# A top-k search on VectorE: two pairs of a head kept aside, and one of its two lists searched past the eighth entry

## Chip, core and metric

The kernel runs on one core of one Trainium2 chip. The metric is device time in microseconds (us) of one execution. The core's engines are TensorE (PE in the profile, with PEld for its weight loads), VectorE (DVE), ScalarE (ACT), GpSimd (POOL) and the DMA queue that SyncE (SP) issues. Each engine works through its own list of instructions in order and waits on semaphores for the others.

## What is computed

The input is 8192 tokens of width 256 (2 sequences of 4096). A first phase is an attention-like layer with layer norms, which the change doesn't touch. The second phase is a layer of product-key experts, and the change lies in its selection of experts. Cut to what matters:

```python
q = (x @ Wq + bq).reshape(B, S, N_HEADS, D_QUERY)            # 8 heads, 64 wide
q1, q2 = q[..., :DQ_HALF], q[..., DQ_HALF:]
s1 = jnp.einsum('bshd,nd->bshn', q1, K1)                     # 64 scores
s2 = jnp.einsum('bshd,nd->bshn', q2, K2)                     # 64 scores
v1, i1 = jax.lax.top_k(s1, TOPK)                             # TOPK = 10
v2, i2 = jax.lax.top_k(s2, TOPK)
all_scores = v1[..., :, None] + v2[..., None, :]             # 10 x 10 sums
all_indices = i1[..., :, None] * N_SQRT + i2[..., None, :]
vals, best = jax.lax.top_k(all_scores, TOPK)
expert_idx = jnp.take_along_axis(all_indices, best, axis=-1)
scores = jax.nn.softmax(vals, axis=-1)
h = jax.nn.gelu(jnp.einsum('bsd,bshkd->bshk', x, W_down[expert_idx]), approximate=False) * scores
out = jnp.einsum('bshk,bshkd->bsd', h, W_up[expert_idx])
```

The experts in use number 4096. The kernel doesn't gather their rows: it multiplies every token with all of them, and with a matrix of gates that is zero where an expert wasn't chosen.

## The kernel before

**Phases.** `attention_phase` runs until about 800 us of the span. `experts_phase` follows and works in 32 chunks of 256 tokens (`C`; two tiles `t` of 128 tokens, `NT` = 2). It is a pipeline over the chunks, written out by hand: in round m (the loops `for m in range(-3, chunks + 1)` of every engine) the engines work on chunk m for the experts' matmuls, on chunk m+1 for the gate matrix, on chunk m+2 for the top-k search, and on chunk m+3 for the queries and scores.

**PE in a round** (lines 1217 to 1237). Sixteen times a `down` (L1201: 12 matmuls, hidden values of 256 experts into PSUM banks `b_ps_h`), and three steps behind it an `up` (L1212: 8 matmuls into `b_ps_a`). Then `turn_x`, `queries` (L1176), `sum_picks` (L1149, needs VectorE's `product`), `scores` (L1186), `turn_picks` (L1157) and four blocks of `gate_matrix` (L1126), each of 128 matmuls with one-hot factors `ohq` and `ohr`. Block b needs `ohr` of that block from VectorE; `ohr` has two buffers, so VectorE may write that of block 2 only once PE is through block 0.

**ACT in a round.** A `gelu` (L1360) for each `down`, one-hots of block 1 (L1339, L1347), then `turn_x`, `keep_gate_parts` (L1316: two copies into a PSUM bank `b_ps_h`, which the factors `ohr` are made from; it has to wait for the last `gelu`), queries, scores (L1298) into `b_score`, the exponential of the softmax (L1304), and the copies of the gate matrix (L1247).

**POOL in a round.** `norm_in` of chunk m+3, then sixteen times a `mix` (L1028: gelu times gates, which `up` of that step waits for) and thirteen times a part of the one-hots of block 0 (L1043). At step 10 come `numbers` (L1059, L1060, the indices of the lists as numbers; it waits for the lists of both tiles) and `pair_numbers` (L1069, L1072, the expert number `cid` of each candidate).

**VectorE in a round** (lines 1612 to 1646). `moments_in`, `decode`; then, for chunk m+2, `lists_first` and `lists_rest` of tile 0 and of tile 1. There are 16 lists of 64 scores (8 heads, two lists each) in a tile. `lists_first` takes the eight largest of each list (L1502) and their indices (L1506). `lists_rest` overwrites these eight (L1513), takes the next eight (L1517) and their indices (L1521), so that ten are known. `pair_sums` (L1540, five instructions) adds the 27 pairs of entries that can be among the ten best into `b_cand`. `pairs_top` does with these 27 what was done with the lists, in five steps of 8 instructions for each tile (L1551, L1555, L1559, L1563, L1567). Then `shift` (L1597), `mask` (L1573, L1581: a comparison over 4320 fp16 elements) and `product` (L1590, the same size, needs `cid`). After that comes chunk m+1: `keep_q_numbers` (L1422), `ohr` of blocks 0 and 1 (L1433, L1438, L1440 each; L1438 waits for `keep_gate_parts`), `ohq` of block 2 (L1412), `finish` (L1480), `ohq` of block 3, `ohr` of block 2 (waits for PE's block 0), `norm_out` (L1489), `ohr` of block 3, `soften` (L1603 to L1607).

The maximum, find-index and match-replace instructions of VectorE work on one list of one head each; find-index and match-replace load the eight values first (MATCH_VALUE_LOAD).

## Time and profile before

| | |
|---|---|
| median of 3 runs | 3499.29 us (3498.52 to 3501.48) |
| the profiled execution | 3501.89 us, its span 3500.1 us |
| mean granted TensorE clock | 0.897 of full speed |
| PE busy | 3179.7 us, 91% of the span |
| DVE busy | 2952.2 us, 84% |
| ACT busy | 2138.9 us, 61% |
| POOL busy | 1916.9 us, 55% |

These shares are means over the attention phase, the two rounds in which the expert pipeline fills, 30 rounds in which all chunks are in work, and the end. Each of these has to be read by itself: which engine's waits end last there. A duration in the trace is that of one instruction from its start to its end; instructions that follow each other on an engine overlap by some 0.1 us, so that a chain of short ones is shorter than the sum of its durations. "issue" as the releaser of a wait means that the profile shows none.

### The profile page before, as it was taken

To read this page: it belongs to the slowest core of one execution; us is meant where nothing else is said; L and a number is where in the kernel's file an instruction comes from. 1 tells how busy PE (TensorE), PEld (TensorE's weight loads), DVE (VectorE), ACT (ScalarE), POOL (GpSimd) and SP (SyncE) were. 2 spreads that over 40 slices of the span, in tenths; PEclk is the share of its full clock that TensorE was granted. 3 is DMA by queue.
4 is the path that set the end of the run, shared out by engine and by line. 5 is a ranking of instruction groups with operands and counts; after the bars stand their busy time and mean duration, and the time that the engine had idled before them with its cause. 6 is when DMAs were issued, how large, how long until landed. Compare 5 with 4: busy or idle time off the path is not lost. (4 is left out here: it accounts for less than half of the span.)

```text
span 3500.1 us, 91378 instructions
## 1 busy us (share of the span) xinstructions
PE 3179.7 (91%) x31284; PEld 2737.6 (78%) x31284; DVE 2952.2 (84%) x15052; ACT 2138.9 (61%) x4475; POOL 1916.9 (55%) x1758
## 2 busy tenths in 40 slices
PE   5999999982499999999999999999999999999998
PEld 3666666641388888888888888888888888888887
DVE  4566666655999999999999999999999999999942
ACT  3444444421677777766766776677667767776762
POOL 1333333332466666665556666666655566666652
PEclk9999999985699999999988899999999889999988
DMA  2111111103333333333333333333333333433332
GB/s 65 49 55 55 55 55 48 45 29 121 125 122 130 119 122 116 107 123 118 107 107 107 124 126 123 121 119 107 116 125 107 107 107 123 127 123 121 116 122 88
DMA packets 132329, 356.86 MB, mean 102 GB/s; under 512 B 13865, under 2 KB 61609, under 8 KB 129452
## 3 DMA queue, kind: packets, MB, share of 16 engines
q1 hardware_dynamic: 131868, 351.03, 31.0%
q8 instruction: 251, 4.11, 0.5%
q14 instruction: 210, 1.72, 0.2%
...
## 5 line engine op out<-in xcount | busy, mean ns | idle before, releaser
L1212 PE MATMUL b_ps_a<-b_wup,b_hid 128*128 128x256 f32 x4096 | 955.7, 379 | 0.0
L1201 PE MATMUL b_ps_h<-b_xT_hi,b_wd_split 128*128 128x256 f32 x4096 | 936.6, 313 | 19.6 <-ACT b_hid L1360 19.5
L1028 POOL TENSOR_TENSOR b_hid<-b_hid,b_gates 128x512 f32<-128x512 f32 x512 | 768.3, 1501 | 182.9 <-ACT b_hid L1360 182.5
L1212 PEld LDWEIGHTS b_ps_a<-b_wup,b_hid 128*128 128x128 f32 x4096 | 744.3, 190 | 84.0
L1201 PEld LDWEIGHTS b_ps_h<-b_xT_hi,b_wd_split 128*128 128x128 f32 x4096 | 707.2, 201 | 35.4 <-issue 24.9
L1339 ACT ACTIVATE b_ohq<-b_q_no,b_minus_qid 80x128 f16<-80x128 f16 x2048 | 648.4, 390 | 1.0
L1201 PE MATMUL b_ps_h<-b_xT_lo,b_wd_split 128*128 128x256 f32 x2048 | 598.9, 292 | 0.0
L1126 PE MATMUL b_ps_s<-b_ohr,b_ohq 80*128 80x32 f16 x16384 | 452.4, 185 | 106.9 <-issue 66.1
L1126 PEld LDWEIGHTS b_ps_s<-b_ohr,b_ohq 80*128 80x128 f16 x16384 | 443.6, 102 | 115.9 <-issue 72.3
L1360 ACT ACTIVATE b_hid<-b_ps_h 128x512 f32<-128x512 f32 x512 | 304.0, 594 | 372.2 <-PE b_ps_h L1201 372.2
L1043 POOL TENSOR_TENSOR b_ohq<-b_qT 80x640 f16<-80x640 f16 (+1 forms) x416 | 520.4, 1252 | 0.0
L1201 PEld LDWEIGHTS b_ps_h<-b_xT_lo,b_wd_split 128*128 128x128 f32 x2048 | 413.9, 202 | 9.9
L1247 ACT ACTIVATE b_gates<-b_ps_s 128x512 f32<-128x512 f32 x512 | 298.4, 596 | 184.7 <-PE b_ps_s L1126 182.0
L1009 POOL TENSOR_SCALAR b_rstd<-b_mv 128x2 f32<-128x2 f32 x64 | 14.1, 221 | 518.1 <-DVE b_mv L1402 518.1
L1347 ACT ACTIVATE b_ohq<-b_ohq,b_one 80x1024 f16<-80x1024 f16 x256 | 291.6, 1139 | 0.0
L1412 DVE TENSOR_TENSOR b_ohq<-b_qid,b_ps_h 80x8192 f16<-80x8192 f16 x64 | 281.4, 4397 | 0.0
L240 POOL TENSOR_TENSOR a_ret<-a_prod 128x512 f32<-128x512 f32 x64 | 84.9, 1327 | 329.6 <-DVE a_prod L618 329.6
L1017 POOL TENSOR_TENSOR b_y<-b_y,b_x1t 128x512 f32<-128x512 f32 x32 | 40.7, 1273 | 303.6 <-DVE b_y L1489 303.6
L1433 DVE TENSOR_TENSOR b_ohr<-b_rid,b_ps_h 80x2048 f16<-80x2048 f16 x128 | 155.2, 1213 | 57.1 <-PE b_ps_s L1126 56.0
L1506 DVE FIND_INDEX8 b_idx<-b_val,b_score 128x8 uint16<-128x64 f32 x1024 | 200.4, 218 | 0.0
L1521 DVE FIND_INDEX8 b_idx<-b_val,b_score 128x8 uint16<-128x64 f32 x1024 | 200.4, 219 | 0.0
L1513 DVE MATCH_REPLACE8 b_score<-b_val,b_score 128x64 f32<-128x64 f32 x1024 | 199.7, 209 | 0.0
...
## 6 DMA issues: line engine op xcount, KB each, us to landing
b_wd_split<-wd_parts SPq DMA_DIRECT2D x512, 512.0 KB, 4.0
...
```

The lines of the kernel that those rows point to most:

```text
L1028: G.tensor_tensor(hid[:, p % 4, :, :], hid[:, p % 4, :, :], gates[:, 2 * p:2 * p + 2, :], ALU.mult).then_inc(mix_done, 1)
L1043: G.tensor_tensor(ohq[:, tok, :].rearrange("p n (a b) -> p n a b", a=16), oh16[:, tok, :].unsqueeze(3).to_broadcast(shape), oh8[:, tok, :] ...
L1126: mm = T.matmul(bank[:, n * NR:(n + 1) * NR], ohq[:, tok, :], ohr[:, b % 2, tok - b * BLK, part, :], start=part == 0, stop=part == 1)
L1201: mm = T.matmul(hbank[p % 2][:, j * C:(j + 1) * C], a, c, start=i == 0, stop=i == len(parts) - 1)
L1212: mm = T.matmul(abank[:, t * D:(t + 1) * D], hid[:, p % 4, j, t * P:(t + 1) * P], wup[:, 2 * p + j, :], start=p == 0 and j == 0 and t == 0 ...
L1247: S.mul(gates[:, :, g * GROUP:(g + 1) * GROUP], sbank[fills["gates", m, g] % 3][:, :].rearrange("p (n r) -> p r n", r=NR), 1.0 / GATE_SCAL ...
L1339: op = S.activation(ohq[:, BLK + i, :], q_no[0:SLOTS, :], ACT.Abs, bias=minus_qid[:, i:i + 1])
L1347: S.activation(rows, rows, ACT.Relu, bias=one[:, :], scale=-1.0).then_inc(ohq_act_done, 1)
L1360: S.activation(hid[:, p % 4, :, :], hbank[p % 2][:, :].rearrange("p (j c) -> p j c", j=2), ACT.Gelu).then_inc(gelu_done, 1)
L1412: V.tensor_tensor(ohq[:, tok, :].rearrange("p n (q s) -> p n q s", s=2), qid[:, tok, :].unsqueeze(2).to_broadcast(shape), q_no_ps.rearrang ...
L1506: op = V.max_index(idx[:, t, l, 0:8], val[:, t, l, 0:8], src(l))
L1521: op = V.max_index(idx[:, t, l, 8:16], val[:, t, l, 8:16], src(l))
```

## The change

On the 16 lists of a tile `lists_first` is unchanged, but both tiles are now done first. A new step `choose` then adds, for each head, the first entry of list 1 and the third of list 2, and the eighth entry of list 1 and the first of list 2, and compares the two sums. By the comparison either list 1 or list 2 of a head is searched further: where it is the second, its scores are copied over those of the first with a predicated copy (64 elements for each of 16 heads and tiles), and its eight values likewise. `lists_rest` then works on 8 lists instead of 16 in a tile. A new step `place_rest` puts the two further entries in the place of both lists and sets them to -3e38 in the one that wasn't searched. POOL's `numbers` waits for it.

`pairs_top` now searches for eight of the 27 pairs only, in two steps instead of five. A new step `sure_pairs` before it takes out two pairs that are certain: the sum of the two first entries, and the larger of the sums (first, second) and (second, first). It writes them into places 8 and 9 of the result and overwrites them in `b_cand`. The order of the ten chosen experts changes by this, which their sum doesn't depend on; `shift` subtracts the value in place 8 instead of that in place 0.

The diff, without empty lines:

```diff
--- before.py
+++ after.py
@@ -37,6 +37,7 @@
 AT_GLO, AT_CID = 5, 10
 ACT_PARTS = 8
 NQ_ACT = NQ
+SURE = 8
 CA = 512
 TA = CA // P
@@ -829,6 +830,8 @@
     id1 = sb("b_id1", [P, HEADS, TOPK, NT], F16)
     id2 = sb("b_id2", [P, HEADS, TOPK, NT], F16)
     cand = sb("b_cand", [P, NT * HEADS, NPAIR], F32)
+    ends, absent, second = cand[:, :, 0:2], cand[:, :, 2:4], cand[:, :, 4].bitcast(mybir.dt.uint32)
     cid = sb("b_cid", [P, HEADS, NPAIR, NT], F16)
     posf = sb("b_posf", [P, SLOTS, NT], F16)
     picked = sb("b_picked", [P, SLOTS, WIDE, NT], F16)
@@ -836,6 +839,7 @@
     pos = picked[:, :, :, :].rearrange("p s c t -> p (s c t)")[:, 0:NT * HEADS * 16].bitcast(U16).rearrange(
         "p (l k) -> p l k", k=16)
     gate = sb("b_gate", [P, NT, SLOTS], F32)
+    won = sb("b_won", [P, NT * HEADS, 2], F32)
     gsum = sb("b_gsum", [P, NT * HEADS], F32)
     ghi = sb("b_ghi", [SLOTS, C, 2], F16)
@@ -894,6 +898,8 @@
     pairs_done = [sem(f"b_pairs{i}") for i in range(NT)]
     ids_done, cand_done, posf_done, mask_done, picks_done = (sem(f"b_{n}") for n in ("ids", "cand", "posf", "mask", "picks"))
     shift_done, gsum_done, grecip_done, gate_done = (sem(f"b_{n}") for n in ("shift", "gsum", "grecip", "gate"))
+    choice_done = sem("b_choice")
+    sure_done = sem("b_sure")
     q_no_done, eid_done, fields_done, qid_done, id16_done, oh16_done = (
         sem(f"b_{n}") for n in ("q_no", "eid", "fields", "qid", "id16", "oh16"))
     ohr_eq_done, ohr_hi_done, ohr_lo_done, ohq_done, q_no_ps_done = (
@@ -1052,8 +1058,7 @@
         def numbers(m):
             i = idx[:, :, :, 0:TOPK].rearrange("p t (h s) k -> p h s k t", s=2)
-            pool.wait_ge(lists_done[0], 5 * (m + 1))
-            pool.wait_ge(lists_done[1], 5 * (m + 1))
+            pool.wait_ge(choice_done, 4 * (m + 1))
             if m:
                 pool.wait_ge(cid_done, m)
             G.tensor_scalar(id1[:, :, :, :], i[:, :, 0, :, :], float(NSQ), -2048.0, ALU.mult, ALU.add)
@@ -1506,20 +1511,53 @@
                 op = V.max_index(idx[:, t, l, 0:8], val[:, t, l, 0:8], src(l))
             op.then_inc(lists_done[t], 1)
+        def choose(m):
+            v = val.rearrange("p t (h s) k -> p (t h) s k", s=2)
+            s = score.rearrange("p t (h s) n -> p (t h) s n", s=2)
+            for t in range(NT):
+                dve.wait_ge(lists_done[t], 5 * m + 2)
+            V.tensor_copy(v[:, :, 0, 8:16], v[:, :, 0, 0:8])
+            V.tensor_tensor(ends[:, :, 0], v[:, :, 0, 0], v[:, :, 1, 2], ALU.add)
+            V.tensor_tensor(ends[:, :, 1], v[:, :, 0, 7], v[:, :, 1, 0], ALU.add).then_inc(choice_done, 1)
+            dve.wait_ge(choice_done, 4 * m + 1)
+            V.tensor_tensor(second, ends[:, :, 0], ends[:, :, 1], ALU.is_ge)
+            V.tensor_tensor(absent[:, :, 0], ends[:, :, 0], ends[:, :, 1], ALU.is_ge)
+            V.tensor_tensor(absent[:, :, 1], ends[:, :, 0], ends[:, :, 1], ALU.is_lt).then_inc(choice_done, 1)
+            dve.wait_ge(choice_done, 4 * m + 2)
+            V.copy_predicated(v[:, :, 0, 8:16], second.unsqueeze(2).to_broadcast([P, NT * HEADS, 8]), v[:, :, 1, 0:8])
+            V.copy_predicated(s[:, :, 0, :], second.unsqueeze(2).to_broadcast([P, NT * HEADS, NSQ]),
+                              s[:, :, 1, :]).then_inc(choice_done, 1)
         def lists_rest(m, t):
-            src = lambda l: score[:, t, l, :]
-            dve.wait_ge(lists_done[t], 5 * m + 2)
-            for l in range(LISTS):
-                op = V.match_replace(src(l), val[:, t, l, 0:8], src(l), GONE)
+            src = lambda h: score[:, t, 2 * h, :]
+            dve.wait_ge(choice_done, 4 * m + 3)
+            for h in range(HEADS):
+                op = V.match_replace(src(h), val[:, t, 2 * h, 8:16], src(h), GONE)
             op.then_inc(lists_done[t], 1)
             dve.wait_ge(lists_done[t], 5 * m + 3)
-            for l in range(LISTS):
-                op = V.max(val[:, t, l, 8:16], src(l))
+            for h in range(HEADS):
+                op = V.max(val[:, t, 2 * h + 1, 8:16], src(h))
             op.then_inc(lists_done[t], 1)
             dve.wait_ge(lists_done[t], 5 * m + 4)
-            for l in range(LISTS):
-                op = V.max_index(idx[:, t, l, 8:16], val[:, t, l, 8:16], src(l))
+            for h in range(HEADS):
+                op = V.max_index(idx[:, t, 2 * h + 1, 8:16], val[:, t, 2 * h + 1, 8:16], src(h))
             op.then_inc(lists_done[t], 1)
+        def place_rest(m):
+            v = val.rearrange("p t (h s) k -> p (t h) s k", s=2)
+            i = idx.rearrange("p t (h s) k -> p (t h) s k", s=2)
+            for t in range(NT):
+                dve.wait_ge(lists_done[t], 5 * m + 5)
+            V.tensor_copy(i[:, :, 0, 8:TOPK], i[:, :, 1, 8:TOPK])
+            for s in range(2):
+                op = V.scalar_tensor_tensor(v[:, :, s, 8:TOPK], absent[:, :, s:s + 1].to_broadcast([P, NT * HEADS, TOPK - 8]), GONE,
+                                            v[:, :, 1, 8:TOPK], ALU.mult, ALU.add)
+            op.then_inc(choice_done, 1)
         def moments_in(m):
             dve.wait_ge(x1_in, 16 * (m + 1))
@@ -1532,48 +1570,53 @@
         def pair_sums(m):
             v = val[:, :, :, :].rearrange("p t (h s) k -> p (t h) s k", s=2)
-            dve.wait_ge(lists_done[0], 5 * (m + 1))
-            dve.wait_ge(lists_done[1], 5 * (m + 1))
-            if m:
-                dve.wait_ge(pairs_done[1], 5 * m)
+            dve.wait_ge(choice_done, 4 * (m + 1))
+            if m:
+                dve.wait_ge(pairs_done[1], 2 * m)
             for a0, na, nb, off in PAIRS:
                 op = V.tensor_tensor(cand[:, :, off:off + na * nb].rearrange("p h (a b) -> p h a b", a=na),
                                      v[:, :, 0, a0:a0 + na].unsqueeze(3).to_broadcast([P, NT * HEADS, na, nb]),
                                      v[:, :, 1, 0:nb].unsqueeze(2).to_broadcast([P, NT * HEADS, na, nb]), ALU.add)
             op.then_inc(cand_done, 1)
+        def sure_pairs(m):
+            first, either = cand[:, :, 0:1], cand[:, :, 1:11:9]
+            s01, s10 = cand[:, :, 1:2], cand[:, :, 10:11]
+            dve.wait_ge(cand_done, m + 1)
+            V.tensor_tensor(won[:, :, 0:1], s01, s10, ALU.is_ge)
+            V.tensor_tensor(won[:, :, 1:2], s01, s10, ALU.is_lt)
+            V.tensor_copy(top[:, :, SURE:SURE + 1], first)
+            V.tensor_tensor(top[:, :, SURE + 1:TOPK], s01, s10, ALU.max).then_inc(sure_done, 1)
+            dve.wait_ge(sure_done, 2 * m + 1)
+            V.memset(first, GONE)
+            V.tensor_scalar(posf[:, :, :].rearrange("p (h k) t -> p t h k", k=TOPK)[:, :, :, SURE + 1],
+                            won[:, :, 0].rearrange("p (t h) -> p t h", t=NT), -9.0, 10.0, ALU.mult, ALU.add)
+            V.scalar_tensor_tensor(either, won[:, :, :], GONE, either, ALU.mult, ALU.add).then_inc(sure_done, 1)
         def pairs_top(m, t):
             src = lambda h: cand[:, t * HEADS + h, :]
             vals = lambda h: top[:, t * HEADS + h, :]
             ids = lambda h: pos[:, t * HEADS + h, :]
-            dve.wait_ge(cand_done, m + 1)
+            dve.wait_ge(sure_done, 2 * m + 2)
             for h in range(HEADS):
                 op = V.max(vals(h)[:, 0:8], src(h))
             op.then_inc(pairs_done[t], 1)
-            dve.wait_ge(pairs_done[t], 5 * m + 1)
+            dve.wait_ge(pairs_done[t], 2 * m + 1)
             for h in range(HEADS):
                 op = V.max_index(ids(h)[:, 0:8], vals(h)[:, 0:8], src(h))
             op.then_inc(pairs_done[t], 1)
-            dve.wait_ge(pairs_done[t], 5 * m + 2)
-            for h in range(HEADS):
-                op = V.match_replace(src(h), vals(h)[:, 0:8], src(h), GONE)
-            op.then_inc(pairs_done[t], 1)
-            dve.wait_ge(pairs_done[t], 5 * m + 3)
-            for h in range(HEADS):
-                op = V.max(vals(h)[:, 8:16], src(h))
-            op.then_inc(pairs_done[t], 1)
-            dve.wait_ge(pairs_done[t], 5 * m + 4)
-            for h in range(HEADS):
-                op = V.max_index(ids(h)[:, 8:16], vals(h)[:, 8:16], src(h))
-            op.then_inc(pairs_done[t], 1)
         def mask(m):
-            dve.wait_ge(pairs_done[NT - 1], 5 * (m + 1))
+            dve.wait_ge(pairs_done[NT - 1], 2 * (m + 1))
             for t in range(NT):
-                op = V.tensor_copy(posf[:, :, t].rearrange("p (h k) -> p h k", h=HEADS),
-                                   pos[:, t * HEADS:(t + 1) * HEADS, 0:TOPK])
+                op = V.tensor_copy(posf[:, :, t].rearrange("p (h k) -> p h k", h=HEADS)[:, :, 0:SURE],
+                                   pos[:, t * HEADS:(t + 1) * HEADS, 0:SURE])
             op.then_inc(posf_done, 1)
             dve.wait_ge(posf_done, m + 1)
+            dve.wait_ge(q_no_done, 1)
             if m:
                 dve.wait_ge(picks_pe, m)
             dve.wait_ge(lists_done[0], 5 * (m + 1))
@@ -1591,11 +1634,11 @@
                 [P, HEADS, TOPK, NPAIR * NT]), ALU.mult).then_inc(picks_done, 1)
         def shift(m):
-            dve.wait_ge(pairs_done[NT - 1], 5 * (m + 1))
+            dve.wait_ge(pairs_done[NT - 1], 2 * (m + 1))
             if m:
                 dve.wait_ge(gate_pe, m)
             V.tensor_tensor(gate[:, :, :].rearrange("p t (h k) -> p (t h) k", k=TOPK), top[:, :, 0:TOPK],
-                            top[:, :, 0:1].to_broadcast([P, NT * HEADS, TOPK]), ALU.subtract).then_inc(shift_done, 1)
+                            top[:, :, SURE:SURE + 1].to_broadcast([P, NT * HEADS, TOPK]), ALU.subtract).then_inc(shift_done, 1)
         def soften(m):
             g4 = gate[:, :, :].rearrange("p t (h k) -> p (t h) k", k=TOPK)
@@ -1607,6 +1650,8 @@
             V.tensor_tensor(g4, g4, gsum[:, :].unsqueeze(2).to_broadcast([P, NT * HEADS, TOPK]), ALU.mult).then_inc(gate_done, 1)
         dve.wait_ge(consts_in, 16 * N_CONSTS)
+        V.memset(posf[:, :, :].rearrange("p (h k) t -> p h k t", k=TOPK)[:, :, SURE, :], 0.0)
         V.tensor_scalar(q_no[:, :], minus_q, -1.0, None, ALU.mult).then_inc(q_no_done, 1)
         for m in range(-3, chunks + 1):
@@ -1616,11 +1661,13 @@
                 decode(m + 1)
             if has(m + 2):
                 lists_first(m + 2, 0)
-            if has(m + 2):
+                lists_first(m + 2, 1)
+                choose(m + 2)
                 lists_rest(m + 2, 0)
-                lists_first(m + 2, 1)
                 lists_rest(m + 2, 1)
+                place_rest(m + 2)
                 pair_sums(m + 2)
+                sure_pairs(m + 2)
                 pairs_top(m + 2, 0)
                 pairs_top(m + 2, 1)
                 shift(m + 2)
```

## Rows read from the trace of the kernel before

**Rows 1.** The page's table of engines: busy us, share of span, instructions.

```profile
PE 3179.7 (91%) x31284; PEld 2737.6 (78%) x31284; DVE 2952.2 (84%) x15052; ACT 2138.9 (61%) x4475; POOL 1916.9 (55%) x1758
```

**Rows 2.** Waits: who waited for whom, us in total, times, longest.

```profile
DVE b_ohr L1433 <- PE b_ps_s L1126: 56.0, 29, 2.0
PE b_ps_s L1126 <- issue: 66.1, 67, 8.4
```

**Rows 3.** Timeline of VectorE, one round: start us, duration us, line, operation.

```profile
2004.70 2.11 DVE L1502 MAX8 b_val<-b_score 128x8 f32<-128x64 f32 x16
...
2010.10 0.09 DVE L1513 MATCH_VALUE_LOAD b_score<-b_val,b_score 128x8 f32 x1
...
2018.62 2.10 DVE L1502 MAX8 b_val<-b_score 128x8 f32<-128x64 f32 x16
...
2032.69 2.00 DVE L1540 TENSOR_TENSOR b_cand<-b_val 128x160 f32<-128x160 f32 x5
2034.73 0.81 DVE L1551 MAX8 b_val<-b_cand 128x8 f32<-128x27 f32 x8
...
2038.33 0.81 DVE L1563 MAX8 b_val<-b_cand 128x8 f32<-128x27 f32 x8
...
2040.43 0.78 DVE L1551 MAX8 b_val<-b_cand 128x8 f32<-128x27 f32 x8
...
2049.27 3.37 DVE L1590 TENSOR_TENSOR b_score<-b_score,b_cid 128x4320 f16<-128x4320 f16 x1
...
2054.06 1.22 DVE L1438 TENSOR_TENSOR b_ohr<-b_ohr,b_ps_h 80x2048 f16<-80x2048 f16 x1
...
2071.68 1.22 DVE L1433 TENSOR_TENSOR b_ohr<-b_rid,b_ps_h 80x2048 f16<-80x2048 f16 x1 [1.93 <-PE b_ps_s L1126]
...
2084.90 2.11 DVE L1502 MAX8 b_val<-b_score 128x8 f32<-128x64 f32 x16
```

**Rows 4.** Timeline of ACT, the second copy of `keep_gate_parts` in that round.

```profile
2053.47 0.36 ACT L1316 COPY b_ps_h<-b_glo 80x256 f32<-80x256 f32 x1
```

**Rows 5.** Timeline of PE in that round, after the last `down`.

```profile
2051.82 5.35 PE L1212 MATMUL b_ps_a<-b_wup,b_hid 128*128 128x256 f32 x24
...
2060.46 2.31 PE L1149 MATMUL b_ps_m<-b_score,b_ident 128*128 128x480 f16 x9
```

**Rows 6.** Timeline of POOL in that round.

```profile
2012.73 1.28 POOL L1028 TENSOR_TENSOR b_hid<-b_hid,b_gates 128x512 f32<-128x512 f32 x1
...
2032.86 1.33 POOL L1043 TENSOR_TENSOR b_ohq<-b_qT 80x640 f16<-80x640 f16 x1
...
2050.54 3.24 POOL L1028 TENSOR_TENSOR b_hid<-b_hid,b_gates 128x512 f32<-128x512 f32 x1 [0.17 <-ACT b_hid L1360]
```

**Rows 7.** One instruction of `pair_sums`, 2033.3 to 2034.0: min/median/max ns.

```profile
L1540 DVE TENSOR_TENSOR b_cand<-b_val x1: 1294/1294/1294, 2033.0 to 2033.0; 128x80 f32<-128x80 f32 x1
```

**Rows 8.** Groups by line of VectorE: xcount, busy us, mean ns, idle before.

```profile
L677 DVE SCALAR_TENSOR_TENSOR a_ph<-a_turns,a_ph 128x1024 f32<-128x1024 f32 x24 | 29.4, 1225 | 0.8
...
L1448 DVE TENSOR_SCALAR b_field<-b_eid 80x64 uint16<-80x64 uint16 x32 | 5.7, 177 | 1.1
```

**Rows 9.** Timeline of VectorE while the pipeline fills.

```profile
853.59 1.18 DVE L1540 TENSOR_TENSOR b_cand<-b_val 128x160 f32<-128x160 f32 x5
...
929.15 2.41 DVE L1590 TENSOR_TENSOR b_score<-b_score,b_cid 128x4320 f16<-128x4320 f16 x1
```

**Rows 10.** Timeline of PE while the pipeline fills.

```profile
871.79 3.78 PE L1149 MATMUL b_ps_m<-b_score,b_ident 128*128 128x480 f16 x9 [28.56 <-DVE b_score L1590]
...
951.48 4.70 PE L1126 MATMUL b_ps_s<-b_ohr,b_ohq 80*128 80x32 f16 x162 [5.31 <-issue]
```

**Rows 11.** Timeline of ACT while the pipeline fills.

```profile
924.38 0.36 ACT L1316 COPY b_ps_h<-b_glo 80x256 f32<-80x256 f32 x1
```

**Rows 12.** Timeline of ACT in the last round with a top-k search.

```profile
3335.40 0.36 ACT L1316 COPY b_ps_h<-b_glo 80x256 f32<-80x256 f32 x1
```

**Rows 13.** Timeline of VectorE in that round.

```profile
3337.52 1.22 DVE L1438 TENSOR_TENSOR b_ohr<-b_ohr,b_ps_h 80x2048 f16<-80x2048 f16 x1
```

## Prediction

> **What bounds the kernel now.** I began with the table of engines [rows 1]: PE is busy for 91% of the span, VectorE for 84%. These are means over stages, and in the expert phase both are near full, so the table decides nothing. The waits do [rows 2]. VectorE waits for PE 29 times, 56.0 us in all: in 29 of the rounds it stands still 1.9 us before `ohr` of block 2, until PE is through block 0 of the gate matrix. PE's own waits in that stage come to 66.1 us "issue" over 67 times, the longest 8.4 us. Then I read one round in VectorE's timeline [rows 3]. It begins its lists at 2004.70 and again at 2084.90, so a round takes 80.20 us. Everything between follows without a gap, except 1.93 us before 2071.68.
>
> That gap is the point to see. VectorE arrives at it early, and leaves it when PE allows. What lies behind it (`ohr` 2, `norm_out`, `ohr` 3) starts from PE's block 0 and not from VectorE's own past. In front of it there is a second tie: the multiplication at 2054.06 needs the copies of ACT, the second of which starts at 2053.47 and takes 0.36, so ends at 2053.83 [rows 3, 4]. VectorE begins 0.23 us after that. However early `product` ends, `ohr` can't be ahead of now by more than 0.23 us, and even this is only added to a wait that exists. `product` itself ends at 2052.64 (2049.27 + 3.37), and PE takes it up at 2060.46, after its queries [rows 3, 5]: 7.8 us of slack. So the filled pipeline runs at PE's pace, with VectorE 1.93 us from being the bound. The search can become some 12 us shorter without a gain there, and may become at most 1.93 us longer.
>
> It is otherwise in three places. While the pipeline fills, PE waits 28.56 us for the first `product` [rows 10]: the whole search of chunk 0 is exposed. In the next round PE waits 5.31 us at block 2, at 951.48, for VectorE, which has worked without a pause since its second search; `product` ended there at 931.56, and ACT's copies at 924.74 [rows 9 to 11], so that tie is far off. In the last round with a search ACT's copies end at 3335.76 and VectorE multiplies at 3337.52 [rows 12, 13]: it is 1.76 us behind, and here nothing waits for PE, since no queries and scores delay PE's block 0.
>
> **The change part by part, without contention.**
> - Removed from the lists: `lists_rest` of a tile takes 8.52 us (2010.10 to 2018.62 [rows 3]), and half of its instructions go. Two tiles: 8.5 us.
> - Removed from the pairs: five steps take 5.70 us a tile (2034.73 to 2040.43), the last two of them 2.10 (2038.33 to 2040.43) [rows 3]. Two steps stay, so 2 x 3.60 = 7.2 us go. Together 15.7.
> - Added: 17 short instructions (7 in `choose`, 3 in `place_rest`, 7 in `sure_pairs`, of 16 to 128 elements) and one predicated copy of 1024 elements. A short one lasts 0.18 us alone, but starts 0.1 us after its forerunner; the nearest row is L1448 with 177 ns [rows 8]. I take 0.12 each, 2.0 us; the ends are 1.3 and 3.0. The wait for its own results that VectorE makes six times costs about 0.12 each, 0.7 us. The trace of before has no predicated copy. L677, with two inputs and 1024 elements, takes 1225 ns [rows 8], and that I take; at two elements a step it would be 0.7, at two passes 2.4. Sum 3.9 us, between 2.7 and 6.1.
> - Net: 15.7 - 3.9 = 11.8 us less in a search, if nothing stands in the way.
> - `lists_first` of tile 1 comes some 8.5 us earlier; its scores were copied in the round before. POOL's `numbers` now waits for `place_rest`, which ends before POOL gets there at its step 10. Behind it stand the `mix` instructions of steps 11 to 15; with contention, below, the two meet within about 1 us, and the `mix` has 3 us or more of slack. The memset ahead of the loop costs nothing that can be read.
>
> **The contention.** One instruction of `pair_sums`, 80 elements, took 1294 ns in the filled pipeline [rows 7], while POOL's one-hots ran from 2032.86 to 2034.19 [rows 6]. All five together took 1.18 us at 853.59, where POOL had little to do, and 2.00 in the round shown [rows 3, 9]. So an instruction with two inputs in SBUF lets the running one of POOL end first, up to 1.2 us, and POOL in turn takes 3.24 us instead of 1.3 for a `mix` that meets `product` [rows 6]. In the part where `choose` falls, from about 2015.4, POOL runs such instructions back to back [rows 6].
>
> The Trainium skill says the same in "SBUF — State Buffer", section "Who interferes with whom": VectorE and GpSimd share a port pair, and "Whoever issues first gets the shared pair for the whole instruction; the other fully blocks". It counts an instruction with two SBUF inputs among those that meet it and a plain copy in a two-port mode too. That speaks against this change, which puts many small ones of this kind where there were few big ones without; taken to its end it gives the first rival below.
>
> About 20 of the instructions in `choose`, `place_rest`, `pair_sums` and `sure_pairs` have two inputs or copy. Between two of POOL's there is a gap of 0.1 us, into which one or two short ones fit. Stepping both queues through with the durations above, I find six waits in `choose`: its copy (0.8), the first sum (1.1), the second with the first comparison (1.0), the other two (1.1), and each predicated copy (1.0), together 6.1. Behind it there are 1.9 in `place_rest`, 1.9 in `pair_sums`, and 1.7 in `mask` and `product`: 11.6 us in all, where before it was 0.8 in `pair_sums` and 1.0 in `product` (3.37 against 2.41 [rows 3, 9]). That eats about 10 of the 11.8 us. `product` then ends 1 to 2 us earlier than now, VectorE waits for ACT's copies or for PE as before, and the round stays at 80.2 us: 30 rounds x 0. POOL's last `mix` ended at 2053.78, while the last 8 of PE's 24 matmuls, which need it, start at about 2055.4 (2051.82 + 5.35 x 16/24) [rows 5, 6]. The two big comparisons now fall before steps 13 and 14 and cost POOL two waits of 2.4; I find 1 us of slack left at step 14.
>
> **The sum.** Chunk 0: POOL is nearly idle after 838, so of 11.8 us one or two waits go (1.3): 10.5 us gained, all of it on the path, since everything up to ACT's second half of preparing weights starts from there. Chunk 1: POOL prepares weights and one-hots back to back, `choose` costs 6.1 more and the rest 1.5: 4.2 us gained (0 to 8.2, the latter up to the tie with ACT's copies). Last search: 1.2 us of the possible 1.76. Together 15.9 us. From the profiled execution's 3501.9 that gives 3486.0; it was 2.6 us above the median of 3499.3, so the forecast for the median is 3484 us with rounding.
>
> **The rivals.**
> - *The port makes VectorE the bound.* If each instruction that meets POOL waits for a whole one, and no two fit in a gap, my steps put the end of `product` 1.1 to 3.7 us later than now. It decides from 1.93 us on, the gap of rows 3, that is from 13.7 us more waiting than now. At 3.2 us late a round costs 1.2 us more, 30 x 1.2 = 36, and the gains left are 10.5 + 0.5: 3499 + 25 = 3524. At the far end (3.7) it is 30 x 1.8 - 10 = 44, 3543. For it: rows 7, a full wait of an instruction that followed another directly. Against it: only one of five waited in that round.
> - *POOL gets late.* With `mask` and `product` ahead of `mix` 13 and 14, `up` waits on PE. If the `mix` is 1 us beyond its slack, 30 x 1 - 15.9 = +14: 3513. It decides from 1 us on.
> - *Nothing at the start either.* If the search of chunk 0 hides another bound (the weights' preparation and its DMAs), 10.5 becomes about 3 and the total is 4 to 6: 3494. The 28.56 us of PE's wait speak against it.
> - *VectorE was the bound.* If the rounds follow VectorE, 1 to 2 us less in 30 rounds give 45 more: 3440. The 29 waits of VectorE for PE speak against it.
>
> **How the numbers follow.** Forecast (fill and end only): 0.68. Port: 0.12. POOL late: 0.07. Nothing at the start: 0.10. VectorE the bound: 0.03. The forecast's own bounds are 3476 (11.8 + 8.2 + 1.8 = 21.8, with 1 us for shorter instructions) and 3492. The range takes in the third rival and small losses in the rounds, up to 0.5 us each: 3476 to 3500. What a measurement can tell from no change is about 0.2%, 7 us. Below 3492.3 lie the forecast and the last rival: 0.70. The third rival and a forecast whose gain is eaten by small losses: 0.14. Slower: 0.16.
>
> **What the profile after would show.** The wait of PE for the first `product` falls from 28.56 to about 18 us; the one at block 2 in the next round from 5.31 to about 2 or 3; rounds still of 80.2 us; VectorE waiting for ACT's copies or PE in each round; three or more of the short instructions of `choose` at over 1 us; the group of `lists_rest` halved. Wrong would be: rounds longer than 80.5, no wait of VectorE before `ohr` 2 (first rival), or PE waiting at L1212 for POOL (second).

## The result, and the profile after

The changed kernel takes 3635.34 us (median of 4 runs, 3634.3 to 3638.24), the kernel before 3499.44 (4 runs, 3498.52 to 3501.48). The ratio is 1.0387, with a 95% interval of 1.0373 to 1.0401: 136 us slower, where 15 us faster was forecast. The first rival happened (the port makes VectorE the bound), at five times its price (136 us against 25): it gave 3524, at its far end 3543.

The page of the changed kernel, its table of engines:

```profile
PE 3180.8 (88%) x31284; PEld 2734.2 (75%) x31284; DVE 3140.7 (86%) x10509; ACT 2138.5 (59%) x4475; POOL 1859.0 (51%) x1758
```

Against [rows 1] PE does the same work in the same time (3180.8 and 3179.7 us). VectorE has 30% fewer instructions (10509 against 15052) and is busy for 189 us more. POOL is busy for less. So short instructions have become long ones on VectorE: one that waits for POOL shows no idle time before it, but a long duration, and counts as busy.

The waits of the changed kernel: who waited for whom, us in total, times, longest.

```profile
PE b_ps_s L1131 <- issue: 182.5, 67, 9.6
DVE b_ohr L1438 <- PE b_ps_s L1131: 2.9, 5, 0.6
PE b_ps_a L1217 <- POOL b_hid L1034: 17.3, 23, 0.8
POOL b_id L1064 <- DVE b_val L1558: 166.8, 32, 11.6
```

These are the mirror image of [rows 2]. VectorE's 29 waits for PE (56.0 us) are down to 5 (2.9 us), and PE's own in the gate stage went from 66.1 to 182.5 us. VectorE had 1.93 us to spare in a round; now PE waits for it. POOL stands before its `numbers` instruction 32 times, 166.8 us in all.

One round in VectorE's timeline (start, duration in us, line, operation), from the first list search to the next, without its own long searches:

```profile
2047.91 2.11 DVE L1507 MAX8 b_val<-b_score 128x8 f32<-128x64 f32 x16
...
2058.64 2.32 DVE L1523 COPY b_val<-b_val 128x128 f32<-128x128 f32 x1
2060.87 1.28 DVE L1524 TENSOR_TENSOR b_cand<-b_val 128x16 f32<-128x16 f32 x1
2062.07 2.55 DVE L1525 TENSOR_TENSOR b_cand<-b_val 128x16 f32<-128x16 f32 x1
2064.66 2.31 DVE L1527 TENSOR_TENSOR b_cand<-b_cand 128x16 uint32<-128x16 f32 x1
2066.88 1.32 DVE L1528 TENSOR_TENSOR b_cand<-b_cand 128x16 f32<-128x16 f32 x1
2068.12 2.56 DVE L1529 TENSOR_TENSOR b_cand<-b_cand 128x16 f32<-128x16 f32 x1
2070.71 2.54 DVE L1531 COPY_PREDICATED b_val<-b_cand,b_val 128x128 f32<-128x128 uint32 x1
2073.15 2.37 DVE L1532 COPY_PREDICATED b_score<-b_cand,b_score 128x1024 f32<-128x1024 uint32 x1
...
2084.53 0.18 DVE L1556 COPY b_idx<-b_idx 128x32 uint16<-128x32 uint16 x1
2084.62 0.29 DVE L1558 SCALAR_TENSOR_TENSOR b_val<-b_cand,b_val 128x32 f32<-128x32 f32 x2
2084.94 1.19 DVE L1577 TENSOR_TENSOR b_cand<-b_val 128x160 f32<-128x160 f32 x5
...
2091.61 2.62 DVE L1640 TENSOR_TENSOR b_gate<-b_val 128x160 f32<-128x160 f32 x1
2094.15 4.97 DVE L1615 CAST b_posf<-b_picked 128x64 f16<-128x64 uint16 x2
2099.16 2.41 DVE L1624 TENSOR_TENSOR b_score<-b_posf,b_pair_no 128x4320 f16<-128x4320 f16 x1
2101.60 2.41 DVE L1633 TENSOR_TENSOR b_score<-b_score,b_cid 128x4320 f16<-128x4320 f16 x1
...
2134.25 2.11 DVE L1507 MAX8 b_val<-b_score 128x8 f32<-128x64 f32 x16
```

The round takes 86.34 us (2134.25 - 2047.91), against 80.20 [rows 3]. The eight instructions of `choose` take 16.9 us (2058.64 to 2075.52); five of them touch 16 elements a partition and last 1.3 or 2.3 to 2.6 us each. Behind `pairs_top`, `shift` (L1640) takes 2.62 us and the two casts of `mask` (L1615) 4.97 us, both unchanged operations, where they take 0.32 and 0.31 while the pipeline fills (at 906.63). `place_rest` and `pair_sums` (2084.53 to 2086.13) wait for nothing. `product` ends at 2104.01, which is 56.1 us after the round's start; before, it was 47.94 (2052.64 - 2004.70, [rows 3]).

POOL's timeline in the same stretch:

```profile
2062.06 1.27 POOL L1049 TENSOR_TENSOR b_ohq<-b_qT 80x640 f16<-80x640 f16 x1
2063.27 1.30 POOL L1034 TENSOR_TENSOR b_hid<-b_hid,b_gates 128x512 f32<-128x512 f32 x1
...
2085.00 0.48 POOL L1064 TENSOR_SCALAR b_id<-b_idx 128x160 f16<-128x160 uint16 x1 [5.74 <-DVE b_val L1558]
...
2094.01 3.81 POOL L1034 TENSOR_TENSOR b_hid<-b_hid,b_gates 128x512 f32<-128x512 f32 x3
```

The second sum (L1525, 2062.07 to 2064.62) starts 0.01 us after a one-hot of POOL, which ends at 2063.33. It doesn't get in there: it lasts until POOL's next instruction, a `mix`, ends at 2064.57. The `numbers` instruction (L1064) has waited 5.74 us for `place_rest`; meanwhile three `mix` instructions have become due, which run back to back from 2094.01 to 2097.82, and POOL's next instruction follows them until 2099.05. The two casts (2094.15 to 2099.12) end with that one.

PE's timeline at the end of the round, block 2 of the gate matrix:

```profile
2124.85 3.58 PE L1131 MATMUL b_ps_s<-b_ohr,b_ohq 80*128 80x32 f16 x128 [5.72 <-issue]
```

VectorE's last multiplication for block 2 ends at 2124.75, and PE, which has stood still for 5.72 us, starts 0.10 us later. In the round of before the same wait was 0.55 us:

```profile
2075.50 3.58 PE L1126 MATMUL b_ps_s<-b_ohr,b_ohq 80*128 80x32 f16 x128 [0.55 <-issue]
```

PE's busy time in the round is 77.48 us against 76.39, at a granted clock of 0.88 against 0.90 of full speed: 5.17 us more of waiting and 1.09 more of work make 6.26, the round's 6.14 within the reading. Whether the lower clock comes from the standing still wasn't tested; it is the small part.

The stretch in which the pipeline fills, PE's timeline, and VectorE's with the start of the third and of the last search:

```profile
808.27 1.11 PE L1144 MATMUL b_ps_m<-b_ident,b_x 128*128 128x128 f32 x4 [24.01 <-POOL b_x L1039]
855.59 3.78 PE L1154 MATMUL b_ps_m<-b_score,b_ident 128*128 128x480 f16 x9 [18.20 <-DVE b_score L1633]
932.93 7.21 PE L1131 MATMUL b_ps_s<-b_ohr,b_ohq 80*128 80x32 f16 x256 [5.39 <-issue]
941.42 2.11 DVE L1507 MAX8 b_val<-b_score 128x8 f32<-128x64 f32 x16
3411.54 2.12 DVE L1507 MAX8 b_val<-b_score 128x8 f32<-128x64 f32 x16
```

PE's wait for the first `product` is 18.20 us, from 28.56 [rows 10]; about 18 was forecast. Block 2 of the next round is reached at 932.93, from 951.48 [rows 10]. The whole account, by the start of the third search and the start of the last:

| | before | after | difference |
|---|---|---|---|
| up to PE's first transposition of the expert stage | 813.78 | 808.27 | -5.5 |
| from there to the third search | 146.2 | 133.2 | -13.0 |
| 29 rounds, third search to last | 2327.2 | 2470.1 | +143.0 |
| from there to the end of the span | 213.0 | 221.0 | +8.0 |
| span | 3500.1 | 3632.5 | +132.4 |

The first line is untouched by the change: over the 13 kernels profiled here it lies between 806.5 and 816.7. So the fill gives 13.0 us, and nearly all of the loss is in the rounds: 4.93 us a round on average, 6.1 in most of them. The 8.0 us at the end have the same source: the last `product` ends 55.69 us after the start of its search, and 48.97 before.

### The profile page after: what moved, and what is told of

Read it like the earlier page. It is cut to its first block, busy times and chain, and to the rows that moved or that the text cites. A ratio compares the mean times of both kernels' runs of the same rounds, so it can differ in the third digit from the quotient of the medians.

```text
span 3632.5 us, 86898 instructions
## 1 busy us (share of the span) xinstructions
PE 3180.8 (88%) x31284; PEld 2734.2 (75%) x31284; DVE 3140.7 (86%) x10509; ACT 2138.5 (59%) x4475; POOL 1859.0 (51%) x1758
## 4 chain that ended last, share of the span: by engine, by line
DVE 39%; issue 18%; POOL 12%; PE 8%; ACT 1%; DVEq 0%; POOLq 0%; DMA 0%; ACTq 0%
POOL b_hid L1034 5%; DVE b_idx L1511 4%; POOL b_ohq L1049 3%; DVE b_ohr L1443 3%; DVE b_ohr L1438 3%; DVE b_ohq L1417 3%; PE b_ps_a L1217 3%; DVE b_posf L1615 2%; DVE b_val L1507 2%; DVE b_idx L1547 2%; DVE b_score L1539 2%; DVE b_picked L1609 1%; PE b_ps_s L1131 1%; DVE b_score L1624 1%; DVE b_val L1531 1%
## 5 line engine op out<-in xcount | busy, mean ns | idle before, releaser
L1217 PE MATMUL b_ps_a<-b_wup,b_hid 128*128 128x256 f32 x4096 | 959.5, 379 | 17.5 <-POOL b_hid L1034 17.3
L1034 POOL TENSOR_TENSOR b_hid<-b_hid,b_gates 128x512 f32<-128x512 f32 x512 | 691.3, 1355 | 122.7 <-ACT b_hid L1365 119.7
L1131 PE MATMUL b_ps_s<-b_ohr,b_ohq 80*128 80x32 f16 x16384 | 453.6, 185 | 228.9 <-issue 182.5
L1049 POOL TENSOR_TENSOR b_ohq<-b_qT 80x640 f16<-80x640 f16 (+1 forms) x416 | 527.0, 1268 | 0.0
L1511 DVE FIND_INDEX8 b_idx<-b_val,b_score 128x8 uint16<-128x64 f32 x1024 | 200.4, 219 | 0.0
L481 ACT COPY a_carry<-a_ps_c 32x512 f32<-32x512 f32 x128 | 68.0, 577 | 210.6 <-PE a_ps_c L337 210.2
L1293 ACT ACTIVATE b_qT<-b_ps_s,b_bq 128x256 f32<-128x256 f32 x128 | 53.7, 471 | 188.6 <-PE b_ps_s L1181 188.6
L1181 PE MATMUL b_ps_s<-b_xT,b_wq 128*128 128x256 f32 x512 | 123.1, 396 | 47.3 <-ACT b_xT L1261 47.3
```

The lines of the kernel that those rows point to most:

```text
L1034: G.tensor_tensor(hid[:, p % 4, :, :], hid[:, p % 4, :, :], gates[:, 2 * p:2 * p + 2, :], ALU.mult).then_inc(mix_done, 1)
L1049: G.tensor_tensor(ohq[:, tok, :].rearrange("p n (a b) -> p n a b", a=16), oh16[:, tok, :].unsqueeze(3).to_broadcast(shape), oh8[:, tok, :] ...
L1131: mm = T.matmul(bank[:, n * NR:(n + 1) * NR], ohq[:, tok, :], ohr[:, b % 2, tok - b * BLK, part, :], start=part == 0, stop=part == 1)
L1181: mm = T.matmul(bank[:, j * C:(j + 1) * C], wq[:, k, n * P:(n + 1) * P], xT[:, k, :], start=k == 0, stop=k == KD - 1)
L1217: mm = T.matmul(abank[:, t * D:(t + 1) * D], hid[:, p % 4, j, t * P:(t + 1) * P], wup[:, 2 * p + j, :], start=p == 0 and j == 0 and t == 0 ...
L1511: op = V.max_index(idx[:, t, l, 0:8], val[:, t, l, 0:8], src(l))
```

## The experiments

**Is it the contention, or the work added? `e1_after_small_onehots` and its control.** POOL's one-hot instructions (527.0 of its 1859.0 busy us in the changed kernel) are cut to one token each in the changed kernel and, as the control, in the kernel before. Both leave out the one-hots of the other tokens, so their gates are wrong; only the time is read.

```diff
+            if m:
+                tok, shape = slice(tok.start, tok.start + 1), [SLOTS, 1, 16, 8]
             G.tensor_tensor(ohq[:, tok, :].rearrange("p n (a b) -> p n a b", a=16),
```

> The changed kernel, in which GpSimd writes only one token of five in each part of its one-hots from chunk 1 on (the rest of block 0 is left as chunk 0 wrote it, so the gates of those tokens are wrong; the time is what is read). Port theory: VectorE's short instructions wait because GpSimd runs back to back. With parts of about 0.3 us in place of 1.26 GpSimd pauses in every step of 3.15 us; the eight instructions of choose fall from 16.9 us to 4 to 8, shift and the two casts of the positions from 7.6 to under 3, and a round goes back from 86.3 to 80.2 us, so the kernel takes 3475 to 3485 us. Rival 1 (the added instructions are dear in themselves, the predicated copies above all): 16.9 and 86.3 stay, 3635 us. Rival 2 (POOL gets to numbers too early and stands there for place_rest, so the mixes behind it are late for PE): rounds stay above 83 us, since the wait for place_rest gets longer when POOL is faster.

> The control: the kernel before with the same cut of GpSimd's one-hots (again the gates of most tokens of block 0 are wrong). All theories: the rounds stay at PE's pace of 80.2 us, 3496 to 3501 us. If it became clearly faster, the one-hots would have bound the kernel before, and the first experiment could not be read as VectorE's contention alone.

Measured: 3478.33 us, ratio to the kernel before 0.9949 (0.9932 to 0.9965), and for the control 3495.4, 0.9997 (0.9988 to 1.0007). VectorE's timeline in a round of the first:

```profile
2077.34 0.51 DVE L1525 COPY b_val<-b_val 128x128 f32<-128x128 f32 x1
...
2078.31 1.17 DVE L1529 TENSOR_TENSOR b_cand<-b_cand 128x16 uint32<-128x16 f32 x1
2079.40 0.44 DVE L1530 TENSOR_TENSOR b_cand<-b_cand 128x16 f32<-128x16 f32 x1
...
2080.18 1.31 DVE L1534 COPY_PREDICATED b_score<-b_cand,b_score 128x1024 f32<-128x1024 uint32 x1
```

`choose` takes 4.1 us instead of 16.9, `product` ends 43.71 us after the round's start (medians here and below), and a round takes 80.17. The same instructions on VectorE, beside a POOL that is busy for less: the change does its work, and the loss is in the waits. One-hots shortened without the change give nothing, so the gain of the first isn't theirs. Its time is about the 3484 that was forecast for the change.

**Which half of the change? `e3_pairs_only` and `e4_lists_only`.** The first keeps the two sure pairs and searches both lists in full (`choose` and `place_rest` out); the second keeps `choose` and gives the pairs their five steps back.

```diff
-                lists_first(m + 2, 1)
-                choose(m + 2)
                 lists_rest(m + 2, 0)
+                lists_first(m + 2, 1)
                 lists_rest(m + 2, 1)
-                place_rest(m + 2)
```

```diff
                 pair_sums(m + 2)
-                sure_pairs(m + 2)
```

> The half of the change on the pairs alone: sure_pairs and two steps instead of five, the lists as in the kernel before. Port theory: 7.2 us go, 1 us is added, sure_pairs meets GpSimd in 2 to 4 places (3 to 5 us), and shift with the two casts, now 4 us earlier, falls among GpSimd's work (5 to 7 us where it was 0.7). product ends 1 to 3 us later than before, of which 1.9 are free: rounds of 80.2 to 81.5 us, 9 us gained while the pipeline fills, 3490 to 3530 us. Rival 1: no contention that matters, 80.2 us a round, 3489 us.

> The half on the lists alone: choose, eight lists instead of sixteen, place_rest; the pairs as before. Port theory: 8.5 us go, 3.1 are added, choose waits 14.2 us for GpSimd. shift and the casts come late, when GpSimd has nothing to do, and cost 0.7 us as before, product 1 us less. product ends 7 us later than before, so rounds of 85 us, 5 to 6 us gained in the fill: 3630 to 3650 us, as slow as the whole change. Rival 1 (shift and the casts carry the loss): 80 to 82 us a round, under 3540 us.

Measured: 3485.4, ratio 0.9963 (0.9949 to 0.9977), for the pairs alone; 3663.36, 1.0475 (1.0456 to 1.0493), for the lists alone. With the pairs alone a round is 80.20 and `product` ends at 47.52; `sure_pairs` takes 1.93, `shift` 1.87 and casts and mask 5.98 us, so here too the tail (`shift`, casts, `mask`, `product`) meets POOL, and the room is used up almost to the 47.94 of before. Both expectations missed: `product` was to end 1 to 3 us later with the pairs alone (3490 to 3530 us) and ends 0.4 earlier; the rounds of the lists alone were to take 85 us (3630 to 3650). With the lists alone `choose` takes 16.86 us, `product` ends at 56.18 and a round takes 86.42. The loss comes with `choose`. That this half is 28 us slower than the whole has three parts: the lists alone gain 4.9 us in the fill instead of 13.0, their rounds are 85.60 us on average against 85.18, 12 us in 29 rounds, and the profiled execution came 7.6 us later to PE's first transposition of the expert stage (815.88 against 808.27), in a stage whose code is the same.

**Which waits? `e5_tail_free`, `e7_choose_free`, `e6_port_free`.** The first leaves `choose` alone and frees the tail: the casts become a `tensor_reduce` over an axis of length one, and `shift` goes behind `product`. The second frees `choose`: its copy and two sums become `tensor_reduce`, and one sum and the predicate lie in free columns of a PSUM bank, so that none of its sums and comparisons has two inputs in SBUF, and the predicated copies take their mask from PSUM. The third is both.

```diff
-                op = V.tensor_copy(posf[:, :, t].rearrange("p (h k) -> p h k", h=HEADS)[:, :, 0:SURE],
-                                   pos[:, t * HEADS:(t + 1) * HEADS, 0:SURE])
+                op = V.tensor_reduce(posf[:, :, t].rearrange("p (h k) -> p h k", h=HEADS)[:, :, 0:SURE],
+                                     pos[:, t * HEADS:(t + 1) * HEADS, 0:SURE].unsqueeze(3), AX.X, ALU.max)
```

```diff
+            row = val.rearrange("p t (h s) k -> p (t h) (s k)", s=2)
+            V.tensor_reduce(v[:, :, 0, 8:16], v[:, :, 0, 0:8].unsqueeze(3), AX.X, ALU.max)
+            V.tensor_reduce(end1, row[:, :, 0:19:18], AX.X, ALU.add)
+            V.tensor_reduce(end2, row[:, :, 7:17:9], AX.X, ALU.add).then_inc(choice_done, 1)
             dve.wait_ge(choice_done, 4 * m + 1)
+            V.tensor_tensor(absent[:, :, 0], end1, end2, ALU.is_ge)
```

> The changed kernel with shift moved behind product, and the two casts of the positions written as a reduction (maximum over an axis of length 1), which has one input and is not a copy. Port theory: the 7.6 us of shift and casts fall to 0.8. But mask and product move up into GpSimd's back-to-back stretch and wait there for 1 to 2 instructions each (1.3 to 5 us together, where the changed kernel has 0 in most rounds). Rounds fall from 85.4 on average to 81 to 84 us: 3500 to 3580 us. Rival (only choose carries the loss, the tail is hidden): 3620 us or more.

> The changed kernel with choose rewritten so that none of its instructions has two inputs in SBUF or is a copy: the copy and the two sums as reductions, one sum and the predicate kept in PSUM. The number and size of the instructions stays 8. The rest is as in the changed kernel. Port theory: choose falls from 16.9 to 3 to 3.5 us. Then place_rest, pair_sums and sure_pairs come 14 us earlier, into GpSimd's back-to-back stretch, where before GpSimd stood waiting for them: 8 to 14 us of new waits there, and 5 to 7 in shift and casts as now. product ends at +53 to +60 us of a round that counts from the lists' start at +4.7 (now 60.8, before 52.6; free up to 54.6): rounds of 80.2 to 85 us, 3480 to 3600 us. Rival 1 (the eight instructions are dear by themselves): choose stays at 13 us or more, 3635 us.

> Both of the above together. Port theory: choose 3 us, shift and casts 0.8, new waits of 8 to 14 us in pair_sums and sure_pairs and 1 to 5 in mask and product; product at +50 to +58: rounds of 80.2 to 83 us, 3478 to 3560 us. Rival (waits of PE for late mixes take over): PE waits at L1217 more than 0.5 us a round.

| | us | ratio (95%) | `choose` | `product` ends | round |
|---|---|---|---|---|---|
| changed kernel | 3635.34 | 1.0387 (1.0373 to 1.0401) | 16.88 | 56.07 | 86.31 |
| tail free | 3591.07 | 1.0251 (1.0222 to 1.0281) | 16.87 | 51.77 | 84.38 |
| `choose` free | 3477.62 | 0.9945 (0.9926 to 0.9964) | 2.52 | 47.50 | 80.17 |
| both free | 3478.77 | 0.9943 (0.9923 to 0.9964) | 2.53 | 43.67 | 80.22 |

(Medians of 26 rounds, without those of fill and end, in us; "ends" is counted from the round's start.) VectorE's timeline in a round of the second:

```profile
2069.21 0.29 DVE L1528 TENSOR_REDUCE b_val<-b_val 128x128 f32<-128x128 f32 x1
2069.41 0.21 DVE L1529 TENSOR_REDUCE b_ps_m<-b_val 128x16 f32<-128x32 f32 x1
...
2069.76 0.19 DVE L1532 TENSOR_TENSOR b_cand<-b_ps_m,b_cand 128x16 f32<-128x16 f32 x1
...
2070.17 0.30 DVE L1536 COPY_PREDICATED b_val<-b_ps_m,b_val 128x128 f32<-128x128 uint32 x1
2070.38 1.36 DVE L1537 COPY_PREDICATED b_score<-b_ps_m,b_score 128x1024 f32<-128x1024 uint32 x1
...
2080.74 4.20 DVE L1561 COPY b_idx<-b_idx 128x32 uint16<-128x32 uint16 x1
...
2085.17 3.06 DVE L1582 TENSOR_TENSOR b_cand<-b_val 128x160 f32<-128x160 f32 x5
...
2094.39 2.29 DVE L1645 TENSOR_TENSOR b_gate<-b_val 128x160 f32<-128x160 f32 x1
2096.61 3.54 DVE L1620 CAST b_posf<-b_picked 128x64 f16<-128x64 uint16 x2
```

`choose` takes 2.5 us with POOL as busy as ever: its instructions run back to back from 2066.52 to 2084.90. Behind `choose` the waits are still there: a copy of 32 elements in `place_rest`, begun 0.80 us after one of POOL's instructions (2079.94), ends only with the third one behind that (2084.90; the copy takes 4.20 us), `pair_sums` takes 3.06, `shift` 2.29, the casts 3.54. But they end within what VectorE has to spare: `product` at 47.50, under the 47.94 of before, and VectorE waits for PE again, 30 times, 60.1 us. (The expectation had 8 to 14 us of new waits and `product` later; `place_rest`, `pair_sums` and `sure_pairs` took 6.5 us more than in the changed kernel, and the time lies just below the 3480 to 3600.) Freeing the tail on top moves `product` 3.8 us ahead and the time by nothing. The waits in `choose` are the cause of the loss. Those of the tail cost nothing without them; on top of them they cost 44 us (3635.34 against 3591.07).

With only the tail freed the round ought to be back to 83.4: VectorE has `shift` behind it at 53.07, which is 5.13 us later than the 47.94 of before, less the 1.93. It is 84.38, above the 81 to 84 expected. Waits in that kernel:

```profile
DVE b_ohr L1438 <- PE b_ps_s L1131: 28.0, 28, 1.0
PE b_ps_a L1217 <- POOL b_hid L1034: 84.6, 78, 1.4
PE b_ps_s L1131 <- issue: 64.8, 67, 8.4
```

PE waits for VectorE no more than before (64.8 us), VectorE again waits for PE before block 2 (28 times, 28.0 us), so it isn't the bound, and PE waits for POOL's `mix` 84.6 us, 78 times. That is the second rival, POOL getting late. It appears here and hardly in the changed kernel (17.3 us), where PE is held up by VectorE first.

**Does an earlier `cid` help? `e8_port_free_cid7`.** The kernel with both parts free, with POOL's `numbers` and `cid` at its step 7 instead of 10.

```diff
-AT_GLO, AT_CID = 5, 10
+AT_GLO, AT_CID = 5, 7
```

> The same with GpSimd's numbers and pair_numbers at its step 7 instead of 10, so that GpSimd reaches them at about the time that place_rest ends, and pair_sums and sure_pairs run beside its short instructions (0.3 to 0.7 us) instead of its 1.25 us ones. Port theory: pair_sums and sure_pairs take under 4 us together, product ends before +47, 7 us before the point from which it costs anything: every round 80.2 us as before, the gain of the fill stays: 3478 to 3486 us, ratio 0.994 to 0.997. Rival: another bound shows in the rounds and takes the gain.

Measured: 3481.48, ratio 0.9948 (0.9932 to 0.9964); `product` ends at 37.99, rounds 80.17. POOL now waits for `place_rest` in each round (32 times, 23.8 us), which therefore meets less of it (0.71 us instead of 4.21), as have `pair_sums` (1.18 instead of 3.05) and `sure_pairs` (1.11). `product` comes 5.7 us earlier than with both parts free, and nothing is gained: as long as VectorE still waits for PE, its own time is free.

**What do further waiters cost? `e9_two_more`.** Two more comparisons of 16 elements in `choose` of the changed kernel, whose results nothing reads.

```diff
             V.tensor_tensor(absent[:, :, 0], ends[:, :, 0], ends[:, :, 1], ALU.is_ge)
+            V.tensor_tensor(extra[:, :, 0], ends[:, :, 0], ends[:, :, 1], ALU.is_ge)
+            V.tensor_tensor(extra[:, :, 1], ends[:, :, 0], ends[:, :, 1], ALU.is_ge)
```

> The changed kernel with two more comparisons of 16 elements in choose, whose results nobody reads. Alone they would take 0.1 us each. Port theory with the measured steps of the changed kernel (an instruction waits out one or two of GpSimd's, 1.28 or 2.55 us): choose 2.5 to 4 us longer, and as VectorE sets the pace of the rounds, all of it in each: 3635 + 29 x 2.5 to 4 = 3700 to 3750 us. Rival (what costs is the number of bytes or the predicated copies, or the semaphore waits): 3635 to 3645 us.

Measured: 3669.98, ratio 1.049 (1.0472 to 1.0507), 35 us over the changed kernel and under the 3700 to 3750 that went with two further full waits in each round. The end of `choose` in one round:

```profile
2086.94 2.54 DVE L1531 TENSOR_TENSOR b_cand<-b_cand 128x16 f32<-128x16 f32 x1
...
2090.73 0.30 DVE L1534 COPY_PREDICATED b_val<-b_cand,b_val 128x128 f32<-128x128 uint32 x1
2090.93 1.31 DVE L1535 COPY_PREDICATED b_score<-b_cand,b_score 128x1024 f32<-128x1024 uint32 x1
```

The two more do wait (seven sums and comparisons now last 1.28 to 2.55 us), but the predicated copies behind them then reach a moment at which POOL pauses (0.30 and 1.31 us instead of 2.54 and 2.37). `choose` is 17.25 us at the median, 0.4 longer, and a round 86.67. That is about 10 us in 29 rounds. The rest comes from elsewhere: the changed kernel has five rounds of 80 to 81 us, this one has none under 85.3 (over all 29, a round is 1.3 us longer). One such round of the changed kernel:

```profile
1722.70 0.18 DVE L1525 TENSOR_TENSOR b_cand<-b_val 128x16 f32<-128x16 f32 x1
1722.91 2.39 DVE L1527 TENSOR_TENSOR b_cand<-b_cand 128x16 uint32<-128x16 f32 x1
1725.22 0.18 DVE L1528 TENSOR_TENSOR b_cand<-b_cand 128x16 f32<-128x16 f32 x1
```

Here the second sum and one comparison get in together with their forerunners (0.18 us each), and `choose` takes 13.3 us. All five short rounds show this order, with 13.0 to 13.9 us. So a wait has no fixed price for each instruction: it depends on how the two queues fall against each other, and a wait may be paid by one instruction or by the next.

**What is a late `product` worth? `e10_before_plus_1us` and `e11_before_plus_4us`.** In the kernel before, two or seven `tensor_reduce` over 512 elements ahead of `mask`: work that VectorE does at the same speed whatever POOL does (675 to 684 ns each in both kernels).

```diff
+                for i in range(2):
+                    V.tensor_reduce(extra[:, i:i + 1], val[:, :, :, :].rearrange("p t l k -> p (t l k)"), AX.X, ALU.max)
                 mask(m + 2)
```

> The kernel before with two more reductions over 512 elements (one input, no contention, about 0.6 us each, results unread) ahead of mask. Theory of the path, as in the prediction: VectorE may become 1.93 us slower in a round without any effect on the rounds of 80.2 us; only the fill gets 2.4 us longer: 3499 to 3503 us, ratio 1.0000 to 1.0015. Rival (VectorE bounds the rounds already): 30 x 1.2 = 36 us more, 3536 us.

> The same with seven such reductions, 4.1 us. Theory of the path: 4.1 - 1.93 = 2.2 us more in each of 29 to 30 rounds, and 8 us in the fill: rounds of 82.4 us, 3499 + 65 + 8 = 3572 us (3555 to 3585). Rival: 30 x 4.1 = 123 us more, 3622 us, or nothing at all if PE alone bounds them, 3507 us.

Measured: 3505.13, ratio 1.0023 (1.0012 to 1.0034), and 3598.87, 1.0286 (1.0269 to 1.0303). `product` ends 2.04 us later in the first, and its round is 80.22, as before; the third search starts 1.1 us later by the mark in the table above, and the end takes 2.6 us longer; the other 3 us of the 7 aren't found in the profiled executions, whose spans differ by 2.8. In the second it ends 5.18 later and the round is 83.36, 3.15 longer. Both came out above their ranges (3499 to 3503, 3555 to 3585): a reduction lasts 0.68 us and not 0.6, and `product` came 2.04 and 5.18 us later where 1.2 and 4.1 were expected. With the gap of 1.93 us from [rows 3]:

| | `product` later than 47.94 | less 1.93 | round longer than 80.21 |
|---|---|---|---|
| two reductions | 2.04 | 0.11 | 0.01 |
| seven reductions | 5.18 | 3.25 | 3.15 |
| changed kernel | 8.13 | 6.20 | 6.10 |
| lists alone | 8.24 | 6.31 | 6.21 |

One rule covers kernels with contention and kernels with plain work. How `product` gets late doesn't matter, only by how much; nothing else in the changed kernel is needed to explain its rounds. It holds there round by round as well, within -0.1 to +0.6 us in 26 rounds, the short ones included. The kernel with the tail free is the exception: with `shift` counted in, its rounds are 1.0 us over the rule; there PE waits for `mix`.

## Why the prediction was wrong

- *The bound and the decision point: right.* VectorE 1.93 us from being the bound, nothing gained in the rounds by a shorter search, every microsecond beyond the gap lost in each round. The table above has it to 0.1 us. So did "the search may become at most 1.93 us longer".
- *Work removed and added, without contention: right.* The added steps cost 3.9 us by the sum; with `choose` freed (in its other form) they are 2.52, with 0.38 for `place_rest` and 1.10 for `sure_pairs` where these don't wait: 4.0. The predicated copy of 1024 elements, bounded by 0.7 and 2.4 and taken at 1.2, is 1.31 to 1.36 us alone.
- *The fill: right but for a detail.* 14.7 us were forecast for chunks 0 and 1, and 13.0 came. PE's first wait is 18.20 (about 18 forecast). The wait at block 2 of the next round is 5.39 and not 2 to 3; PE comes to it earlier by as much. So the third rival (nothing at the start) and the fourth (VectorE was the bound) didn't happen. The 1.2 us at the end didn't come: the end is 8.0 us longer, by the same waits.
- *The waits in `choose`: the first term that failed.* The working let a waiting instruction lose one of POOL's, at most 1.2 us, and let two short ones slip into each gap: six waits, 6.1 us. Measured: 16.88 us against the 2.52 of the freed one, 14.4 us of waits. In the round shown all eight instructions wait, five of them until the second of POOL's has ended. The one row at hand [rows 7] showed a wait of one, and this was taken for the rule. The gap of 0.1 us between two of POOL's instructions stands in no row either: the trace has each start some 0.04 us before the end of the one in front (2062.06 + 1.27 against 2063.27). In the five short rounds two short instructions do get in behind their forerunners; in the round shown, as in most, none does.
- *The tail: the second term.* `place_rest`, `pair_sums`, `mask` and `product` were given 5.5 us of waits. The changed kernel has none in the first two and 6.9 elsewhere: `shift` 2.28 (2.61 - 0.33) and the casts 4.65 (4.97 - 0.32). These two were left out of the step-through, as unchanged. They are, but the change moved them to where POOL is busy; before, they took 0.33 and 0.32 us.
- *"The two meet within about 1 us": the third.* POOL's `numbers` waits 5.7 us for `place_rest`. It gives `place_rest` and `pair_sums` an idle POOL, and the casts meet the `mix` instructions held up by it. How much of their 4.97 us is due to that wasn't tested apart: with `choose` free, where POOL doesn't wait in this place, they still take 3.54. A wait of one queue on the other was costed for who waits, not for what it moves.
- *Slips that decide nothing.* The six waits listed for `choose` add up to 6.0 us, not 6.1. The two rivals that make the kernel slower have 0.19 together, while "slower" was given 0.16.

Together: 11.6 us of waits were forecast and 21.3 came (14.4 + 6.9). Less the 1.8 that were there before, and less the 11.8 saved, that puts `product` 7.7 us later; 8.1 was measured. Forecast and fact are 9.7 us apart by these two terms. The first rival knew the mechanism, the place and the point from which it decides; its size, 1.1 to 3.7 us later, had the same flaw as the forecast: one of POOL's instructions as the most that a wait can last. With two for each, its six waits would be 1.3 us longer each, 7.8 in all, and its range 8.9 to 11.5 instead of 1.1 to 3.7; between the two lies the 8.1 that came. The chance of 0.12 was too small as well, since forecast and rival both hung on a count of gaps that no row could show.

The Trainium skill, in "SBUF — State Buffer", section "Who interferes with whom", says that whoever issues first has the shared ports for the whole instruction and the other blocks. The rows agree in who waits: the sums and comparisons with two inputs in SBUF do, for 1.28 to 2.55 us in place of 0.18. They differ in how long: the second sum, begun at 2062.07, also sat out the `mix` that began at 2063.27, after it, and the measurement decides. The section also says that `tensor_reduce` never contends on this chip; the trace agrees, with 0.29 us for 128 elements beside a busy POOL.

What stays open: why a waiting instruction sits out two of POOL's and not one, and by which rule two, one, two follow each other in `choose`, both in its copy and two sums (2.32, 1.28, 2.55 us) and in its three comparisons (2.31, 1.32, 2.56 us). It repeats in most rounds, so it is hardly chance; no run here tells whether it is the grant of the ports or the time between VectorE's instructions that decides it.
